# ScalarE fetches 11 of 831 edge tiles row by row on its own DMA queue, in place of gathers by GpSimd

## The reference

```
seg = edge_dst * R + edge_type
S   = segment_sum(h[edge_src], seg, N * R).reshape(N, R, D)
cnt = segment_sum(ones, seg, N * R).reshape(N, R)
agg = einsum('nrd,rdf->nf', S, relation_weights) + cnt @ rFeatures
h   = agg * deg ** -0.5                 # deg: edges into each node, at least 1
out = layernorm(x + relu(h + h @ loop_weight))
```

## Time and profile before

| | |
|---|---|
| time, median of 3 runs | 1070.57 us (1070.49 to 1072.32) |
| profiled execution, span from first to last instruction | 1067.5 us |
| median of the runs above the profiled span | 3.1 us |
| mean granted clock of PE | 0.990 of full speed |
| PE, DVE, ACT, POOL busy | 89%, 69%, 50%, 74% of the span |
| gathers by POOL (plain blocks, from x_parts) | 85, 736 |
| rows by SP | 1162 |

### The profile page before, as it was taken

How to read it: one execution, slowest core, us unless ns; L and a number is a source line. 1 busy time by engine, 2 the same in 40 slices (tenths; PEclk the granted TensorE clock), 3 DMA queues, 4 the chain that set the end, 5 groups by cost and what they waited for, 6 DMA issues and landing times.

```text
span 1067.5 us, 28985 instructions
## 1 busy us (share of the span) xinstructions
PE 954.3 (89%) x6713; PEld 852.9 (80%) x6713; DVE 741.5 (69%) x2588; ACT 531.6 (50%) x1137; POOL 789.4 (74%) x836
## 2 busy tenths in 40 slices
PE   2589999998999999999988999999899999999997
PEld 0378888887888888888878888888788888888887
DVE  6698877666767676667667666766667676767673
ACT  1576655444454454545454454455445544544551
POOL 7777777777777777777777777777777777777770
PEclk9799999999999999999999999999999999999999
DMA  5952334434333333434434434333333334333330
GB/s 165 296 190 56 89 110 118 115 113 118 114 113 115 116 115 115 115 114 118 115 114 115 117 112 116 113 112 112 115 112 112 113 111 115 112 112 112 114 110 24
DMA packets 64548, 125.18 MB, mean 117 GB/s; under 512 B 16835, under 2 KB 36006, under 8 KB 64374
## 3 DMA queue, kind: packets, MB, share of 16 engines
q0 software_dynamic: 38048, 102.09, 33.3%
q1 hardware_dynamic: 12294, 14.85, 4.2%
q10 hardware_dynamic: 14032, 6.35, 2.0%
HBM read 113.62 MB, written 9.60 MB: 115 GB/s over the span
## 4 chain that ended last, share of the span: by engine, by line
PE 45%; DMA 27%; POOL 13%; issue 8%; DVE 1%; POOLq 0%; ACT 0%; ACTq 0%; DVEq 0%; SPq 0%
DMA rows<-x_parts,src 27%; PE win_ps L1003 23%; PE agg_ps L1015 19%; POOL rows L505 13%; PE win_ps L1088 1%; PE win_ps L1041 1%; PE win_ps L992 1%; POOL raw L512 1%; DMA x_in<-x 0%; PE win_ps L1040 0%; POOLq L504 0%; DMA raw<-x,src 0%; ACT ring L595 0%; POOLq L117 0%; DVE ring L897 0%
## 5 line engine op out<-in xcount | busy, mean ns | idle before, releaser
L505 POOL DMA_INDIRECT rows<-x_parts,src x736 | 698.2, 949 | 224.3 <-issue 153.9
L595 ACT COPY ring<-win_ps 128x451 f32 x831 | 465.2, 560 | 362.9 <-PE win_ps L1003 206.7
L1003 PE MATMUL win_ps<-hot,rows 128*128 128x480 f32 x1642 | 563.1, 428 | 71.7 <-DMA rows<-x_parts,src 64.6
L1015 PEld LDWEIGHTS agg_ps<-ring,w 128*128 128x128 f32 x3936 | 551.2, 191 | 40.9
L1015 PE MATMUL agg_ps<-ring,w 128*128 128x128 f32 x3936 | 559.5, 274 | 0.0
L795 DVE TENSOR_SCALAR hot<-iota,key_f 128x480 fp32r<-128x480 f16 x831 | 392.6, 473 | 0.8 <-issue 0.8
L897 DVE TENSOR_TENSOR ring<-ring,win_ps 128x41 f32 x831 | 188.0, 226 | 293.7 <-DMA rows<-x_parts,src 234.3
L1003 PEld LDWEIGHTS win_ps<-hot,rows 128*128 128x128 f32 x1642 | 252.7, 192 | 114.8 <-DMA rows<-x_parts,src 103.4
L512 POOL DMA_INDIRECT raw<-x,src x85 | 89.3, 1051 | 25.9 <-issue 20.7
L992 PEld LDWEIGHTS win_ps<-hot_node,hot_type 128*128 128x128 bf16 x831 | 79.7, 99 | 33.3 <-issue 15.1
L992 PE MATMUL win_ps<-hot_node,hot_type 128*128 128x12 bf16 x831 | 85.4, 170 | 21.0 <-DVE ring L897 12.7
(11 more groups left out here) (87 smaller groups left out, 259.5 us busy)
## 6 DMA issues: line engine op xcount, KB each, us to landing
x_out<-x_parts SPq DMA_DIRECT2D x1162, 1.0 KB
rows<-x_parts,src POOLq DMA_INDIRECT x736
x_parts<-x_out SPq DMA_DIRECT2D x12, 512.0 KB, 3.3
x_in<-x SPq DMA_DIRECT2D x12, 256.0 KB, 4.4
out<-out_sb ACTq DMA_DIRECT2D x48, 64.0 KB
x_blk<-x ACTq DMA_DIRECT2D x47, 64.0 KB
w<-relation_w SPq DMA_DIRECT2D x8, 320.0 KB
raw<-x,src POOLq DMA_INDIRECT x85
```

The source lines that it names most:

```text
L505: pool.indirect_dma_start(rows[0:n, k].rearrange("p c d -> p (c d)").bitcast(F32), None, x_parts, bass.IndirectOffsetOnAxis(ap=src[0:n, t: ...
L595: nc.scalar.copy(ring[:, :, bass.ds(start + 1, WIN - 1)], win_ps[bank_of(t)][:, :, 1:WIN]).then_inc(copied, 1)
L1003: ins = nc.tensor.matmul(banks[bank_of(t)][:, 0:R * WIN], of[:, part], hot[:, t % HOTS], start=False, stop=(part == PARTS - 1), skip_group ...
L1015: ins = nc.tensor.matmul(sums_of(c), w[:, r, :], ring[:, r, bass.ds(seg, BLOCK)], start=(r == 0), stop=(r == COLS - 1))
```

## The change

A second list, BY_ACT, holds tile 12 of blocks 8, 12, ..., 48: 11 tiles. POOL leaves them out, and DVE counts POOL's gathers without them. ACT fetches their rows from x_parts: beginning four blocks ahead, it issues two row transfers behind each copy of a tile's sums, and a load of four indices before every second pair, so that the 128 rows of a tile are issued over 64 of the 68 tiles of four blocks. The indices are loaded at the start as one 11 x 128 array and multiplied by 1024 on DVE, so that ACT has a byte address without arithmetic. SP's row buffers become six, and the two that it gives up are ACT's. PE waits for the semaphore of the tile's own transfers.

```diff
-BY_ROW_BUFS = 8
+BY_ROW_BUFS = 6
+ACT_FROM = 4
+ACT_ROWS = 2
+ACT_BLOCKS = 4
+ACT_TILE = 12
+BY_ACT = [i * TPB + ACT_TILE for i in range(ACT_FROM + ACT_BLOCKS, BLOCKS, ACT_BLOCKS)]
+ACT_BUFS = 2
+ACT_LOAD = 4
+ROW_BYTES = 2 * D * 4
...
+        by_act = by_row[:, BY_ROW_BUFS:BY_ROW_BUFS + ACT_BUFS]
+        act_src = sb("act_src", [len(BY_ACT), P], I32)
+        act_at = sb("act_at", [len(BY_ACT), P], I32)
+        x_bytes = x_parts.bitcast(U8).rearrange("n b -> (n b)").unsqueeze(0)
...
-            return len([n for n in range(k, t + 1, TPB) if n not in BY_ROW])
+            return len([n for n in range(k, t + 1, TPB) if n not in BY_ROW and n not in BY_ACT])
...
+            sp.dma_start(act_src[:], src_by_tile[BY_ACT[0]:BY_ACT[-1] + 1:ACT_BLOCKS * TPB, :]).then_inc(act_src_loaded, 16)
...
-                if t in BY_ROW:
+                if t in BY_ROW or t in BY_ACT:
...
+            index = [act.alloc_register(f"act_row{n}") for n in range(ACT_LOAD)]
+
+            def fetch(i, k):
+
+                j, part = divmod(i - ACT_FROM, ACT_BLOCKS)
+                if j < 0 or j >= len(BY_ACT):
+                    return
+                first = (part * TPB + k) * ACT_ROWS
+                if first == 0:
+                    if j == 0:
+                        act.wait_ge(act_ready, 1)
+                        for h in range(2):
+                            act.wait_ge(staged[h], len(range(h, STAGES, 2)) * 16)
+                    if j >= ACT_BUFS:
+                        act.wait_ge(tile_done, BY_ACT[j - ACT_BUFS] + 1)
+                for p in range(first, min(first + ACT_ROWS, P)):
+                    if p % ACT_LOAD == 0:
+                        act.load(index, act_at[j:j + 1, p:p + ACT_LOAD])
+                    at = act.snap(index[p % ACT_LOAD])
+                    act.dma_start(by_act[p:p + 1, j % ACT_BUFS].rearrange("p c d -> p (c d)").bitcast(U8),
+                                  x_bytes[:, bass.ds(at, ROW_BYTES)]).then_inc(by_act_landed[j], 16)
...
                         nc.scalar.copy(ring[:, :, bass.ds(start + 1, WIN - 1)],
                                        win_ps[bank_of(t)][:, :, 1:WIN]).then_inc(copied, 1)
+                        fetch(i, k)
...
-                        dve.wait_ge(gather_issued, last + 1 - len([n for n in BY_ROW if n <= last]))
+                        dve.wait_ge(gather_issued, last + 1 - len([n for n in BY_ROW + BY_ACT if n <= last]))
...
+                dve.wait_ge(act_src_loaded, 16)
+                nc.vector.tensor_scalar(act_at[:], act_src[:], float(ROW_BYTES), None, ALU.mult).then_inc(act_ready, 1)
...
+                    elif t in BY_ACT:
+                        pe.wait_ge(by_act_landed[BY_ACT.index(t)], P * 16)
...
-                of = by_row[:, BY_ROW.index(t) % BY_ROW_BUFS] if t in BY_ROW else rows[:, k]
+                if t in BY_ROW:
+                    of = by_row[:, BY_ROW.index(t) % BY_ROW_BUFS]
+                elif t in BY_ACT:
+                    of = by_act[:, BY_ACT.index(t) % ACT_BUFS]
+                else:
+                    of = rows[:, k]
```

More of the change, by code:

```diff
@@ L11 @@
 I32 = mybir.dt.int32
+U8 = mybir.dt.uint8
 F32R = mybir.dt.float32r
@@ L89 @@
 assert STAGED_FIRST + sum(len(v) for v in STAGE_AT.values()) == STAGES and PLAIN_BLOCKS >= 4
+assert ACT_ROWS * ACT_BLOCKS * TPB >= P and P % ACT_LOAD == 0 and BY_ACT[-1] < FULL and not set(BY_ACT) & set(BY_ROW)
 assert USED > LAST * TPB + SUMS_FROM and R % W_LOAD == 0 and FREE_W % W_LOAD == 0
@@ L267, in build @@
         by_row_src_loaded = [sem(f"by_row_src_loaded{j}") for j in range(len(BY_ROW))]
+        act_src_loaded = sem("act_src_loaded")
+        act_ready = sem("act_ready")
+        by_act_landed = [sem(f"by_act_landed{j}") for j in range(len(BY_ACT))]
         by_row_landed = [sem(f"by_row_landed{j}") for j in range(len(BY_ROW))]
```

## The result

The changed kernel takes 1349.95 us (median of 4 runs, 1348.59 to 1351.23) where the kernel before takes 1070.53 (4 runs): a ratio of 1.2608, 95% interval 1.2591 to 1.2626. The loss is 280 us, four times the 70 that were forecast; the value lies outside the range. The profiled span is 1347.8 us, the mean granted clock of PE 0.922.

The account below looks back on a forecast made before the run. POOL's 821 gathers were taken to bound the kernel before; after the change ACT's queue would, 986 us of work against 910.7: +75, less 5 given back, on 1067.5 makes 1137.5, plus 3.1 is 1141 us, range 1068 to 1190.

Parts of the forecast that it names:

- pairs: Sign in ACT's queue: copies in pairs of about 1.02 and 1.36 us, with the idle before them put to issue.
- One row: ACT's queue: each row transfer costs 0.40 us, priced from SP's rows (bounds 0.265 to 0.51); 1408 make 563 us.
- One index load: ACT's queue: a load of up to four indices costs 0.335 us with its gap; 352 make 118 us.
- The copies' steps: ACT's queue around copies: 704 x 0.22 = 155 us, plus 29 us for the 40 tiles without rows.
- the large transfers: ACT's queue: two big transfers a block, with small copies and roots, 1.1 x 43.8 = 48 us.
- What stands there already: ACT's existing queue work: 219 position loads at 0.335, 73 us, and big transfers with small copies and roots, 48 us.
- The tail: The 19 tiles after the last row took 23.1 us; going faster, they give back 5 us (0 to 8).
- Rival 1: ACT's queue: rows fit beside copies and waits, so POOL's 11 gathers less count, 1057 us; chance 0.14.
- Rival 2: ACT's queue: rows partly hidden at 0.35 to 0.38 us each, about 1090 us; chance 0.08.
- Rival 3: SP and ACT share the generator and delay each other's issues: +40 us, 1181 us; chance 0.08.
- Rival 4: ACT's waits for DVE stay: +43 us if a third is kept, 1183 us, all +127; chance 0.08.
- Rival 5: ACT's row transfers are cut over 16 engines: +150 us or more, about 1290 us; chance 0.02.

Follow-up runs that it names:

- e5: The changed kernel without ACT's row transfers and index loads, PE multiplying what lies in the buffers: 1057.64 us (kernel before 1070.10), ratio 0.9885.
- f4: The changed kernel with four indices loaded once a tile and used for all its rows (wrong rows in 11 tiles): 1134.51 us.
- e6: The changed kernel with ACT's rows from fixed addresses, so without index loads and moves: 1064.82 us (kernel before 1070.10).
- e2: The changed kernel with ACT's row addresses written as SP's, in words: 1564.99 us on a chip where the kernel before took 1385.35.
- f1: The changed kernel with one row behind each copy and five tiles by ACT: 1066.76 us (kernel before 1070.17), ratio 0.9973.
- e7: The changed kernel with eight indices loaded right behind the position load of every fourth tile: 1344.52 us (kernel before 1070.10).
- e3: The changed kernel with 16 indices a load: 1524.85 us on a chip where the kernel before took 1385.35.
- f2: The changed kernel, all 11 tiles, with 16 indices a load and 16 positions a load: 1184.28 us.
- e11: The changed kernel with five tiles by ACT, one row a copy, wide loads, 15 tiles by SP: 1657.17 us (kernel before 1392.08), ratio 1.1896.
- f3: Same program as e11 on another chip, compared with the kernel before: 1062.10 us (1070.17), ratio 0.9917.
- e9: Same program as f1 on another chip, compared with the kernel before: 1407.02 us (1392.08), ratio 1.0108.

## Why the prediction was right and wrong

**What bounds the kernel.** Right: the gathers of POOL do (e5 gives 12.5 us for eleven, forecast 13.8), and the change makes ACT's queue the bound. The direction and the mechanism held, the size did not: +282.3 us in ACT's stretch in place of +75. Most signs named for it came: pairs (1.00 us without a load, 1.65 with one and a small copy, where 1.36 was named), idle time put to issue, real waits of POOL, no wait for var_eps. One seems not to have: the view still puts 185.8 us of ACT's idle time to PE. That is a naming, not a wait. The copy at 507.74 has 1.08 us put to PE, while ACT's queue issued and loaded until 507.50; and all pauses over 0.1 us in ACT's queue add up to about 40 us in the stretch, in the kernel before to about 600. A block is 27.96 us long (fin_sb copied at 500.70 and at 528.66), 27.3 on average, not 22.5.

**The ledger.** The copies of the earlier trace rows in the changed kernel, blocks 4 to 47 to tile 12, and all:

```profile
L634 ACT COPY ring<-win_ps x744: 534/569/598, 111.5 to 1304.5; 128x451 f32 x186
...
L634 ACT COPY ring<-win_ps x831: 526/568/601, 26.9 to 1324.7; 128x451 f32 x167
```

The stretch takes 1193.0 us. Summed over the records of ACT's queue in that stretch (rounded; the copies' item holds what was waited there):

| item | forecast | measured |
|---|---|---|
| rows | 1408 x 0.40 = 563 | 1408 x 0.471 = 664 |
| index loads | 352 x 0.335 = 118 | 352 x 0.46 = 162 |
| position loads | 219 x 0.335 = 73 | 125 |
| between them, with the copies' own steps | 155 + 29 = 184 | about 200 |
| two large transfers a block, and small copies | 48 | about 41 |
| sum | 986 | about 1192 |

**The step that failed** is the pricing of *One row* and *One index load*: both prices came from stretches that do only one of the two. The five rows of SP in the earlier trace rows follow each other with no load between; ACT's loads of the earlier trace rows never had a row ahead. Each price is right where that holds (0.386 us from one row to the next, 0.40 forecast; 0.310 for a load behind a load, 0.307 forecast). Where they alternate, the row behind a load takes 0.233 more, about 105 us for 451 of them, and a load behind a row 0.17 to 0.28 more at the medians, some 96 us over index and position loads. Together that is the 200 us by which the sum was short. f4 takes away 341 loads and so about half of the alternation: 215 us go, 100 more than at the forecast's price. The other half, around the position loads, stays. The copies' steps were 16 short, the large transfers 7 over. A row's mean, 0.471, lies inside the bounds that the prediction gave it (0.265 to 0.51); but its time range used 0.39 to 0.416 only, and the loads had no bounds at all.

The trace of the kernel before had little to warn of it. Its loads behind large transfers take 0.308, so they show nothing. The one sign was on SP, whose queue does load between its rows, 16 indices at a time: the row behind such a load takes 0.270 in place of 0.225. That is a fifth of what ACT then paid.

**The position loads** show a second slip: they were entered as *What stands there already*, at their old price. An instruction that the change does not touch was costed as untouched, though its neighbour was new.

**The tail.** The 19 tiles behind the stretch took 20.2 us instead of 23.1: 2.9 given back, 5 forecast. The forecast's own row, 19 tiles at 1.06 us, gives 3; its 5 did not follow from it.

**The rivals.** Rival 1 (hidden, 1057) is what happens without the queue's work, in e5: 1057.64. Its threshold, 0.337 us a row, rested on the forecast's prices for all else; with what these measured it would be (897 - 162 - 125 - 200 - 41) / 1408 = 0.26. e6, at 0.31 but without index loads, does not test it. Rival 2 (a row at 0.35 to 0.38) did not come. Rival 3 (SP and ACT share the generator) fell: SP ends at 666.2 us in the changed kernel, and the median of the first row behind a load is 0.467 or 0.468 before and after; their mean is 0.477 while SP issues and 0.468 after, 2 us in all where 40 were named. Rival 4 (ACT's waits for DVE) fell: 29.5 us, put to issue. Rival 5 (a row in pieces, 1290) was nearest in time, by luck, and wrong in cause: the issues are 234 ns, and a row of ACT is one packet of 1024 bytes and one of 4.

The Trainium skill, DMA: Bandwidth & Descriptors, section Issuing engines are not separate DMA queues, holds the starter's own time "usually small relative to the DMA itself". The trace agrees for a single row: its issue takes 0.234 or 0.467 us, and its packet of 1 KB ends 1.03 us (median) after the issue began. But what counts here is how many starts one queue can make. To take the sentence as a reason to leave the 563 us out would have given a win of 13 us; measured, the row starts are 664 of the 1193 us in which ACT's queue sets the time. The same page, section Latency and other measured facts, gives a floor of about 600 ns for a load into a register. As a floor it does not hold here: four registers take 0.31 us behind another load, and behind rows 0.46 to 0.74 (medians 0.48 for index loads, 0.57 for position loads). As a price it would have served a little better: an estimate with 0.6 and a gap of 0.03 gives 571 loads 360 us, where the forecast had 191 and 287 were measured.

## What to carry to other kernels

Price an engine's instruction queue as well as its busy time, and price each queue instruction by a row in which it has the neighbour that it will have: a load between transfers, a transfer behind a load. Where the nearest row comes from a stretch that does one kind only, take it as a lower bound and not as a mean. A queue that looks idle takes work cheaply up to the point where it is full: with five tiles the kernel was 3.4 us faster, with eleven 280 us slower, so try half of it first, and load many indices at a time, at starts that divide evenly.

## What the runs showed of the hardware

- On ACT, a row transfer behind a register load takes 0.467 us instead of 0.234, with byte, word or fixed addresses (the changed kernel, e2, e6), and a load of up to four registers behind a row 0.46 to 0.74 instead of 0.31. One row since the last load is enough (f1: 0.477 or more in all 70 such loads); one large transfer is not (0.308 in the kernel before). On SP, whose loads bring 16 indices, the first row behind a load takes 0.270 instead of 0.225, so it is not the same on each engine. What in the chip does it, these runs don't show.
- Behind a position load, a load of eight registers takes 0.547 us when it starts at an index divisible by four, and 1.74 to 1.79 when only by two; a load of two registers takes 0.50 from either (e7).
- A load of 16 registers on ACT takes 1.03 us behind another load and 1.2 behind rows (e3, f2).
- PE's granted clock averages 0.99 while POOL sets the pace and 0.922 in the changed kernel, in which PE waits more between bursts. PE has 76% busy time there and is not the bound; no run shows a cost of it.
- The same kernel took 1070 us on two chips and 1385 and 1392 on two others; e11 lost 19% where f3, the same program, won 0.8%, and e9 lost 1.1% where f1 won 0.3%. Why the chips differ is not shown. A ranking of kernels that live from issue time need not carry over from chip to chip.
